# Two chained 3x3 convolutions: the intermediate on 48 partitions of each half by two queues, TensorE's waits a unit ahead, halos copied three units ahead

## What is computed

```
x = x + conv3x3(groupnorm(x), W0) + b0     # 4 groups of 2 channels, over all rows and columns
x = x + conv3x3(groupnorm(x), W1) + b1
```

## Time and profile before

| | us |
|---|---|
| median of 3 runs | 4213.01 (4202.11 to 4214.97) |
| the profiled execution | 4238.59 |
| its span, from first to last instruction | 4236.8 |
| TensorE busy | 3712.5 |
| VectorE busy | 2026.7 |
| ScalarE busy | 1763.8 |
| GpSimd busy | 1363.6 |

### The profile page before, as it was taken

One profiled execution on the slowest core, in us unless ns is written; L12 is line 12 of the kernel. 1 busy time (PEld: TensorE's weight loads), 2 busy tenths in 40 slices (PEclk: granted clock), 3 DMA queues, 4 the chain that ended last, 5 costly groups with the idle time before them and its releaser, 6 DMA issues.

```text
span 4236.8 us, 87949 instructions
## 1 busy us (share of the span) xinstructions
PE 3712.5 (88%) x33232; PEld 1551.0 (37%) x33232; DVE 2026.7 (48%) x3110; ACT 1763.8 (42%) x1381; POOL 1363.6 (32%) x1829
## 2 busy tenths in 40 slices
PE   0087877898889999998889999999999999999999
PEld 0032322353333333353333333345564333343333
DVE  6866666565564444445556344444445222332222
ACT  0032222343334555533333555544443555555554
POOL 0011111111113545521111444441211555555555
PEclk9999898999999999999999999999999999999999
DMA  9989999999999999999999999999999999999997
GB/s 323 392 290 392 387 390 380 354 379 379 380 383 303 343 368 379 338 346 381 376 376 351 303 350 368 337 287 373 357 357 317 283 293 288 282 273 292 289 279 226
DMA packets 367108, 1435.02 MB, mean 339 GB/s; under 512 B 49888, under 2 KB 50016, under 8 KB 334176
## 3 DMA queue, kind: packets, MB, share of 16 engines
q10 hardware_dynamic: 176736, 627.30, 48.4%
q0 software_dynamic: 153344, 536.96, 33.5%
q1 hardware_dynamic: 36864, 268.45, 16.9%
HBM read 895.64 MB, written 536.87 MB: 338 GB/s over the span
## 4 chain that ended last, share of the span: by engine, by line
PE 56%; ACTq 12%; issue 12%; DMA 11%; DVE 6%; ACT 1%; POOL 1%; POOLq 0%; DVEq 0%; SPq 0%
PE conv L632 56%; ACTq L479 12%; DMA out_dram<-out_tile 8%; DMA stat_tile<-x_dram 2%; DVE bn_x L681 2%; ACT out_tile L465 1%; DVE out_tile L708 1%; DVE bn_mid L691 1%; POOL x_tile L405 1%; DMA mid_dram<-out_tile 1%; DVE mv_mid L719 1%; POOL out_dram L385 0%; DVEq L681 0%; DVE mv_x L713 0%; POOLq L385 0%
## 5 line engine op out<-in xcount | busy, mean ns | idle before, releaser
L632 PE MATMUL conv<-x_tile,wts 64*64 64x512 f32 x32832 | 3694.7, 600 | 281.2 <-ACT out_tile L465 190.0
L632 PEld LDWEIGHTS conv<-x_tile,wts 64*64 64x64 f32 x32832 | 1530.7, 135 | 2426.2 <-issue 2363.6
L465 ACT ACTIVATE out_tile<-conv,bias 128x1024 f32<-128x1024 f32 x688 | 729.1, 1111 | 1351.2 <-PE conv L632 749.6
L691 DVE BATCH_NORM_STATS2 bn_mid<-out_tile 128x512 f32 (+1 forms) x1376 | 849.5, 680 | 886.1 <-ACT out_tile L465 885.9
L708 DVE TENSOR_SCALAR out_tile<-conv,bias 128x1024 f32<-128x1024 f32 x340 | 436.4, 1283 | 1253.9 <-PE conv L632 1093.9
L371 POOL DMA_DIRECT2D mid_dram<-out_tile x680 | 344.7, 508 | 1712.2 <-ACT out_tile L465 1658.8
L470 ACT ACTIVATE out_tile<-conv,bias 128x1024 f32<-128x1024 f32 x344 | 383.5, 1115 | 831.9 <-PE conv L632 690.0
L508 ACT ACTIVATE x_tile<-x_tile 16x2048 f32<-16x2048 f32 x340 | 648.7, 1908 | 56.7 <-issue 37.4
L681 DVE BATCH_NORM_STATS2 bn_x<-stat_tile 128x512 f32 (+1 forms) x1024 | 629.1, 678 | 49.6 <-DMA stat_tile<-x_dram 49.4
L405 POOL COPY x_tile<-x_tile 16x2048 f32<-16x2048 f32 x340 | 639.8, 1882 | 1.6
L385 POOL DMA_DIRECT2D out_dram<-out_tile x680 | 349.9, 516 | 899.1 <-DVE out_tile L708 830.3
(11 more groups left out here) (62 smaller groups left out, 115.7 us busy)
## 6 DMA issues: line engine op xcount, KB each, us to landing
x_tile<-x_dram ACTq DMA_DIRECT2D x680, 512.0 KB, 22.7
stat_tile<-x_dram SPq DMA_DIRECT2D x256, 1024.0 KB, 9.9
out_dram<-out_tile POOLq DMA_DIRECT2D x680, 384.0 KB, 7.8
mid_dram<-out_tile POOLq DMA_DIRECT2D x672, 384.0 KB, 9.4
x_tile<-mid_dram ACTq DMA_DIRECT2D x340, 640.0 KB, 6.5
x_tile<-mid_dram ACTq DMA_DIRECT2D x344, 128.0 KB, 8.7
mid_dram<-out_tile POOLq DMA_DIRECT2D x8, 416.0 KB, 10.0
x_tile<-x_dram ACTq DMA_DIRECT2D x8, 256.0 KB
```

Of the source, the lines that this page charges most:

```text
L465: last = act.activation(out_tile[0:parts, slot, i], conv[0:parts, bank, i], ACT.Identity, bias=bias0[0:parts, win.parity, int(unit.last), ...
L632: last = nc.tensor.matmul(to, weights, x_tile[HALF * half:HALF * (half + 1), slot, middle, c + kw:c + kw + BANK], start=(kw == 0), stop=(k ...
L691: last = dve.bn_stats(bn_mid[0:parts, unit.win.pair % 2, i, bass.ds(unit.n * 2 + h, 1), :] .rearrange("p a b -> p (a b)"), out_tile[0:part ...
```

## The change

It has three parts.

- **Partitions and queues.** A unit of layer 1 reads 48 partitions (16 to 63) by ScalarE's queue and 48 (80 to 127) by SyncE's; both halves now use the same `PLACES`. The first halo is copied from partitions 96 to 111, the second to 64 to 79. The edge rows and the last unit stay on ScalarE's queue. SyncE, before its half for unit u+8, waits until TensorE has finished unit u (`conv_done`) and until GpSimd has taken the next unit's first halo; its statistics tiles come behind that in its own order. ScalarE keeps the wait for the first halo only where it loads rows of layer 0 into a slot of layer 1.
- **TensorE's waits.** The waits for unit u+1 are put into unit u, in its second half of columns: for rows, edge and pads before `kw` 0, for the halos before `kw` 1, for the bank (the eviction of unit u-1) before `kw` 2. Each group ends with a count on a semaphore that nobody waits for. It holds in both layers.
- **Halos.** GpSimd and ScalarE copy them for the unit three after the one just evicted instead of two.

The diff, without unchanged parts:

```diff
--- before.py
+++ after.py
@@ -65,13 +65,13 @@
 
 FIRST, SECOND, LAST_BAND = range(3)
 BLOCKS0 = (((8, 0, 1), (16, 1, 2), (32, 5, 2), (48, 3, 2)),
-           ((0, 5, 2), (16, 1, 2), (32, 3, 2)),
+           ((0, 1, 2), (16, 5, 2), (32, 3, 2)),
            ((16, 5, 2), (48, 7, 1)))
 
-PLACES = ((0, 8, 16, 24, 48, 56, 32, 40), (32, 40, 16, 24, 48, 56, 0, 8))
+PLACES = (0, 8, 16, 24, 48, 56, 32, 40)
 
 TAKEN_IN = (range(ROWS_IN), range(1, ROWS_IN), range(LAST_ROWS + 1))
-MID_PARTS = 80
+BAND_PARTS = CH * ROWS_OUT
 
 assert LAST_ROWS == 4 and TAIL <= UNITS - 18
 
@@ -231,6 +231,7 @@
         stored_last = sem("stored_last")
         stat_loaded = [sem(f"stat_loaded{s}") for s in range(STAT_SLOTS)]
         stat_used = sem("stat_used")
+        slots_free = sem("slots_free")
         edge_loaded = sem("edge_loaded")
         first_halo, second_halo = sem("first_halo"), sem("second_halo")
         unit_begun, results_seen = sem("unit_begun"), sem("results_seen")
@@ -255,6 +256,19 @@
 
             return same_layer_before(unit.win) * UNITS + unit.n
 
+        def load_mid(queue, unit, part, first, rows, done):
+
+            both = mid[unit.win.image:unit.win.image + 2, bass.ds(first, rows), :]
+            queue.dma_start(x_tile[part:part + rows, unit.slot, :, 1:SIDE + 1],
+                            both.rearrange("n r w -> r n w")).then_inc(done, 16)
+
+        def wait_for_mid(queue, win):
+
+            done = next(v.w for v in WINDOWS if v.layer == 0 and v.pair == win.pair) + 1
+            for s in range(RING):
+                queue.wait_ge(stored[s], 32 * len(range(s, done * UNITS, RING)))
+            queue.wait_ge(stored_last, 16 * last_stores(done))
+
 
         AGGREGATE, MEAN, VAR, ROOT, WEIGHTS = (TAIL + X_RING + d for d in (0, 4, 5, 6, 7))
         BIAS = WEIGHTS + 2
@@ -273,6 +287,19 @@
 
             def window(win):
                 def step(unit, in_loop):
+                    following = unit.after(X_RING)
+                    if following is not None and following.win.layer == 1 and not following.last:
+                        if following.b == 0:
+                            wait_for_mid(sp, following.win)
+                        sp.wait_ge(conv_done, unit.count + 1)
+                        sp.sem_inc(slots_free)
+                        neighbour = unit.after(1)
+                        if win.layer == 1 and neighbour is not None and neighbour.win is win:
+                            sp.wait_ge(first_halo, halos_through(neighbour))
+                            sp.sem_inc(slots_free)
+                        load_mid(sp, following, HALF + PAIR,
+                                 following.n * OUT_ROWS + (CH + BAND_PARTS), BAND_PARTS,
+                                 x_loaded[following.slot])
                     if not in_loop and unit.b == HEAD - 1 and win.x_each:
                         for i in range(STAT_SLOTS):
                             load_stat(win.x_pair, win.x_first + i, i,
@@ -324,7 +351,7 @@
                 for row in range(1, ROWS_OUT + 1):
                     alone(pool.affine_select(
                         ident1[half, VALID + row - 1:VALID + CH * ROWS_OUT:ROWS_OUT],
-                        one[half, 0:CH], [[-1, CH]], ALU.is_equal, 0.0, -PLACES[i][row], 1))
+                        one[half, 0:CH], [[-1, CH]], ALU.is_equal, 0.0, -PLACES[row], 1))
             alone(pool.affine_select(own_group[:, 0, 0], one[:, 0:BOTH], [[-2 * ROWS_IN, BOTH]],
                                      ALU.is_ge, 0.0, 0, 1))
             alone(pool.affine_select(own_group[:, 0, 0], own_group[:, 0, 0], [[2 * ROWS_IN, BOTH]],
@@ -403,7 +430,8 @@
                 pool.sem_inc(results_seen)
                 pool.wait_ge(pads_written, pads[0])
                 pool.tensor_copy(x_tile[0:PAIR, unit.slot, :, 1:SIDE + 1],
-                                 x_tile[HALF:HALF + PAIR, earlier.slot, :, 1:SIDE + 1]) \
+                                 x_tile[HALF + 2 * PAIR:HALF + 3 * PAIR, earlier.slot, :,
+                                        1:SIDE + 1]) \
                     .then_inc(first_halo, 1)
                 if isinstance(unit.n, int):
                     copied[0] = halos_through(unit)
@@ -423,7 +451,7 @@
                         if copied[0]:
                             pool.wait_ge(first_halo, copied[0])
                         write_pads(following)
-                    following = unit.after(2)
+                    following = unit.after(3)
                     if following is not None and following.win.layer == 1 and following.b:
                         copy_first_halo(following)
 
@@ -444,7 +472,7 @@
                                   taps[0, :, :, columns]).then_inc(setup_loaded, 16)
                 for i, kind in ((0, INNER), (0, TOP), (0, BOTTOM), (1, INNER)):
                     if r in TAKEN_IN[kind]:
-                        place = HALF * i + PLACES[i][r]
+                        place = HALF * i + PLACES[r]
                         act.dma_start(rows1[place:place + CH, kind, :, CH * lo:CH * hi],
                                       taps[1, :, :, columns]).then_inc(setup_loaded, 16)
 
@@ -487,35 +515,20 @@
                             .then_inc(x_loaded[slot], 16)
                     return
 
-                def load_rows(part, first, rows, done):
-                    both = mid[win.image:win.image + 2, bass.ds(first, rows), :]
-                    act.dma_start(x_tile[part:part + rows, slot, :, 1:SIDE + 1],
-                                  both.rearrange("n r w -> r n w")).then_inc(done, 16)
-
                 first = unit.n * OUT_ROWS + CH
                 if unit.last:
-                    load_rows(PAIR, first, PAIR, x_loaded[slot])
-                    load_rows(3 * PAIR, first + PAIR, CH, x_loaded[slot])
+                    load_mid(act, unit, PAIR, first, PAIR, x_loaded[slot])
+                    load_mid(act, unit, 3 * PAIR, first + PAIR, CH, x_loaded[slot])
                     return
                 if unit.kind == TOP:
-                    load_rows(CH, 0, CH, edge_loaded)
-                load_rows(VALID, first, MID_PARTS, x_loaded[slot])
-                load_rows(P - PAIR, first + MID_PARTS, PAIR, x_loaded[slot])
-
+                    load_mid(act, unit, CH, 0, CH, edge_loaded)
+                load_mid(act, unit, PAIR, first, BAND_PARTS, x_loaded[slot])
             def copy_second_halo(unit):
 
                 act.wait_ge(x_loaded[unit.slot], (unit.turn + 1) * 32)
-                act.activation(x_tile[HALF + HALF // 2:HALF + HALF // 2 + PAIR, unit.slot, :,
-                                      1:SIDE + 1],
-                               x_tile[HALF // 2:HALF // 2 + PAIR, unit.slot, :, 1:SIDE + 1],
+                act.activation(x_tile[HALF:HALF + PAIR, unit.slot, :, 1:SIDE + 1],
+                               x_tile[2 * PAIR:3 * PAIR, unit.slot, :, 1:SIDE + 1],
                                ACT.Identity).then_inc(second_halo, 1)
-
-            def wait_for_mid(win):
-
-                done = next(v.w for v in WINDOWS if v.layer == 0 and v.pair == win.pair) + 1
-                for s in range(RING):
-                    act.wait_ge(stored[s], 32 * len(range(s, done * UNITS, RING)))
-                act.wait_ge(stored_last, 16 * last_stores(done))
 
             def take_root(n):
                 act.wait_ge(var_read, n + 1)
@@ -534,12 +547,13 @@
                     following = unit.after(X_RING)
                     if following is not None:
                         if following.b == 0 and following.win.layer == 1:
-                            wait_for_mid(following.win)
+                            wait_for_mid(act, following.win)
                         neighbour = unit.after(1)
-                        if win.layer == 1 and neighbour is not None and neighbour.win is win:
+                        if win.layer == 1 and following.win.layer == 0 and neighbour is not None \
+                                and neighbour.win is win:
                             act.wait_ge(first_halo, halos_through(neighbour))
                         load(following)
-                    following = unit.after(2)
+                    following = unit.after(3)
                     if following is not None and following.win.layer == 1 and not following.last:
                         copy_second_halo(following)
 
@@ -595,28 +609,49 @@
                                                     bias_col[0:HALF, 1:2], start=False, stop=True)
                 last.then_inc(bias_summed, 1)
 
-            def wait_for_bank(earlier):
+            def wait_for_rows(unit):
+
+                if unit.win.layer == 0 or unit.last:
+                    pe.wait_ge(x_loaded[unit.slot], (unit.turn + 1) * 32)
+                if unit.win.layer == 1 and unit.kind == TOP:
+                    pe.wait_ge(edge_loaded, 16 * (same_layer_before(unit.win) + 1))
+                if isinstance(unit.n, int) and unit.n < X_RING:
+                    pe.wait_ge(pads_written, unit.win.w * X_RING + unit.n + 1)
```

(40 more changed lines are left out.)

## The result

The changed kernel takes 4235.96 us in the median of 7 runs (4227.98 to 4256.58), the kernel before beside it 4213.05 (4192.49 to 4219.74, 7 runs): ratio 1.006, 95% interval 1.0037 to 1.0084. The forecast was 4151. The profiled execution of the changed kernel took 4236.84 us (span 4235.2), close to its median; that of before lies 25.6 us over its own. So the two traces are equally long (spans 4235.2 and 4236.8) though the medians lie 23 us apart, and they have to be compared by stretches.

The account below looks back on a forecast made before the run. No single bound: the late halo copy in layer 1 without statistics, the DMA beside statistics tiles. Halos -65, moved tiles +8 and -5 sum to -62, so 4213 became 4151 us; range 4112 to 4187.

Parts of the forecast that it names:

- The bound by window: Windows 6 and 7 wait for the halo copy, 0.27 us a unit; layer 1 and layer 0 with statistics are DMA-bound.
- Halos three ahead, -65 us: Layer 1: earlier copies and waits bring units to 5.15 us; loops 30, first units 11, last 20 intervals 24 us.
- The upper bound of 71: Layer 1 halo term: the most it was thought to gain, in us, if the loop's exit step goes wholly.
- Two queues for the intermediate ... so this is worth 0: Layer 1 loads: ScalarE issues one transfer a unit instead of two; landing time and five-unit lead suffice; 0 us.
- What moves on SyncE's queue, +8 (bounds -6 to +31) and -5: Four tiles, 4.19 MB, move into windows 2 and 4, +4 us each; ends of windows 1 and 3 gain 5 together.
- Layer 0, 0 us: TensorE's waits a unit ahead in layer 0: delays hidden by the full DMA, no wait for rows expected; 0 us.
- rival D: Layer 0 windows pay 56 us in full for TensorE's earlier waits, so no change: 4207 us; chance 0.06.
- Rival E: TensorE's late start is the string of waits itself, not the copy; loops stay at 5.42: 4203 us; chance 0.07.
- Rival B: Saturated stretches gain too: stores are served more often, land sooner, evictions stop waiting for them: 4122 us; chance 0.25.
- Rival C: Windows 2 and 4: halves behind tiles on SyncE's queue land late, halo copies wait, 7.4 us a unit: 4335; chance 0.07.
- point of decision of 6.3: Rival C, windows 2 and 4: above 6.3 us a unit, 114 units eat up the 70 us gained.

Follow-up runs that it names:

- e5: Kernel before with halos copied three units ahead alone, old loads and TensorE's waits as before: 4150.16 us, ratio 0.9825.
- e3: Kernel before with TensorE's moved waits and halos three ahead, old loads of 80 and 16 partitions on ScalarE's queue: 4150.75 us, ratio 0.9843.
- e2: Changed kernel with both 48-partition halves on ScalarE's queue and SyncE free to run ahead: 4156.84 us, ratio 0.984.
- e4: Kernel before with TensorE's waits a unit ahead alone, loads and halos (two ahead) as before: 4874.02 us, ratio 1.1546.
- e1: Changed kernel, but SyncE issues the first four statistics tiles of windows 1 to 4 from unit 73 of the window before: 4225.43 us, ratio 0.9999.
- e11: e2, but SyncE waits for the end of unit 8 before the first four tiles of windows 2 and 4: 4174.57 us, ratio 0.9876.
- e9: Kernel before with the loads split into 48 and 48 partitions on two queues alone, halos two ahead, TensorE's waits as before: 4291.39 us, ratio 1.016.
- e12: Kernel before with halos three ahead and a pair's two images side by side in the DRAM intermediate: 4273.28 us, ratio 1.0134.
- e14: Kernel before with halos three ahead and statistics tiles read in 4 KB runs instead of 8 KB: 4110.68 us, ratio 0.9748.
- e10: Changed kernel with the second half on SyncE's queue in windows 6 and 7 alone, both halves on ScalarE's queue below that: 4152.89 us, ratio 0.9865.
- e7: Changed kernel with both 48-partition loads of layer 1 on SyncE's queue, in order with the statistics tiles: 4245.25 us, ratio 1.0051.
- e15: Changed kernel with statistics tiles read in 4 KB runs instead of 8 KB: 4221.92 us, ratio 1.0002.
- e17: Changed kernel with second half on GpSimd's store queue, ScalarE's half as two transfers, SyncE's queue for tiles alone and early: 4204.61 us, ratio 0.9972.
- e8: Changed kernel with layer 1 units loaded whole, even ones by ScalarE's queue and odd ones by SyncE's: 4230.72 us, ratio 1.0027.
- e13: Changed kernel with a pair's two images side by side in the DRAM intermediate: 4342.8 us, ratio 1.0288.

## Why the prediction was wrong, step by step

- **The bound by window** was right. Windows 6 and 7 wait for the halo copy, windows 2 and 4 for the DMA.
- **Halos three ahead, -65 us**: right in mechanism and, for the loops, the first 8 units and the exit, in size (294, 41 and 104 us). The ends of the four windows were taken too low: 24 us, where the last 20 intervals of windows 2, 4, 6 and 7 gave 37 us between the two profiles (112 to 103, 114 to 102, 115 to 107, 110 to 103) and 29 us in e5. e5 gives the sum alone: 1.75% of 4221 is 74 us, e3 and e2 1.6%, 66 to 68. The upper bound of 71 doesn't add up: all 8 us in four windows make 73. The step claimed the gain for both edits; TensorE's moved waits add nothing and are harmful without the other (e4).
- **"Two queues for the intermediate ... so this is worth 0": this step failed.** It priced issue time, landing time and lead, all of which were covered, and took the rate at which the DMA serves as given. The rate fell from 366 and 356 GB/s to 343 and 332. Priced by runs, the split takes the ratio from 0.984 (e2) to 1.006, 2.2% or 93 us: some 26 us of it the shift of the tiles (e1 against the changed kernel; e11 against e2 says 18, not clear of the noise), the other 67 the split itself (e1 against e2).
- **What moves on SyncE's queue, +8 (bounds -6 to +31) and -5**: the bytes were right (123 MB), but both terms were too small. In e11, where the burst stands alone, it cost the loops 41 us, beyond the +31, and gave back 21 at the ends. The upper bound took "the window's own rates" as the worst. They are the rates of another arrangement of queues, and no bound: in the changed kernel the loops took 37 and 40 us more, split and shift together, and the ends of windows 1 and 3 12 us less.
- **Layer 0, 0 us**: about right, but not for the reason given. "No wait for them shows before" was said of the rows of x; now TensorE waits for them 39 times, 51.2 us, 40.0 of it in window 0, while its waits for ScalarE's eviction fell from 190.0 to 148.3. Every kernel with the moved waits has such waits for rows of x, and none of the others has (before, e5, e9, e12, e14). Window 0's loop was 11 us longer in this profile; e10, with the same waits, has 414 us as before. So **rival D** (56 us) is wrong in size, and whether a few microseconds of it are real stays open.
- **Rival E** falls: the loops of windows 6 and 7 came to 294 us.
- **Rival B** is wrong in sign. Stores do get more turns (37.8% of the time against 35.4% in the whole loop of before), but each costs more, and they land in 19.2 us instead of 16.0. The rule cited there tells who is served, not how fast. A rule of the Trainium skill that speaks against the change was left out (DMA: Bandwidth & Descriptors, Rules for kernel authors): it advises one transfer over two to disjoint halves, and says that spreading over issuing engines doesn't help bandwidth. The runs agree and go further: beside tiles it hurts.
- **Rival C** named the right place (SyncE's queue, windows 2 and 4) and the right sign, but not the mechanism. In the changed kernel no halo copy waits for rows (halves on SyncE's queue land in 9.4 us); only in e7 and e15 do they to any extent. The loops' 6.30 and 6.49 us a unit lie near its point of decision of 6.3, which is chance. I gave it 0.07 because its mechanism could not last; the place deserved more than the mechanism.

By stretches, the two profiles differ by the halos' -78 us, +76 in the loops of windows 2 and 4, +14 in window 0, -12 at the ends of windows 1 and 3, which makes about 0. The medians differ by +23. The difference fits the profiled execution of before, which was 25.6 us slower than its median; in which stretch, one trace can't tell.

What stays open is why a DMA engine takes longer over the same packets. Measured in the loops of windows 2 and 4 are: half of the rows on the stores' queue (e17, 350 GB/s), all rows and tiles in one ordered queue (e7, 323 and 329), rows on two queues, one of them the tiles' (changed kernel, e1, e8, e9, e13, e15: 328 to 343), rows on one queue and tiles on another (356 to 373, once 348 in e11; with 4 KB tiles 374 and 381). Each number is from one profile. Ruled out as the cause are the partitions (e2), simultaneous halves (e8) and the place of the two images in DRAM (e13); the tiles' packet size alone isn't it either (e15, with its reservation). That each further queue in flight costs something would be the nearest reading, but e7, with the fewest queues and the lowest rate, speaks against it.

## What to carry to other kernels

Before a transfer is moved to another queue, ask which transfers share the DMA engines at that time, and price the rate as an unknown of its own: a stretch whose DMA share is 1.0 has a rate that depends on how the streams are arranged, and the rate of the present arrangement bounds nothing. If a copy or halo ends just as it is needed, start it a step earlier and try that alone; two integers gave the whole gain here. When a change joins several edits, cost each one alone: here one gave 1.75% and another, with the shift that it brings, took 2.2%.

## What the runs showed of the hardware

- DMA share near 1.0 says little of the rate: 290 GB/s at 0.99 in window 6 of before, 305 at 1.01 after, 323 at 1.02 in e7, 390 at 1.03 in e14. In the first two the DMA isn't even the bound: TensorE waits for the halo copy there (309 us a loop), and after the change it is busy throughout (294).
- Beside other traffic, transfers in packets of 8 KB went with a lower rate in all than the same bytes in packets of 4 KB: layer 0 with statistics 359 instead of 383 GB/s (window 0, e12 against e5; the partitions of a store and its place in DRAM changed with them), layer 1 with statistics 361 and 364 instead of 374 and 381 (e5 against e14; the rows of a partition changed with them). In windows 1 and 3, smaller tile packets gained nothing (386 and 388 before, 383 and 390 after).
- In GpSimd's queue, half of the rows behind the stores (e17) cost less than in SyncE's behind the tiles: 350 against 331 and 342 GB/s (e1, tiles early in both).
